# Rope attention: the first two maxima tiles of a step stand between the scores of the two head pairs

## The chip, the cores and the metric

The kernel runs on one core of a Trainium2 chip as one program. The metric is the time of one execution on the device in microseconds (us); before the change it was 4140.08 us (median of three runs, 4134.7 to 4146.66).

## What is computed

Six blocks follow one another on 4 sequences of 1024 tokens of width 128: a feed-forward with rope attention and routed experts, a linear attention, the first kind of feed-forward again, then two mixtures of 14 experts around a causal attention. The change touches the rope attention, which runs twice (blocks one and three). Cut to it:

```
q = (src @ Wq).reshape(Bb, Tt, H, DH).transpose(0, 2, 1, 3)          # H = 16 heads, DH = 8
k = (src @ Wk_c @ Wk).reshape(Bb, Tt, H, DH).transpose(0, 2, 1, 3)
v = (src @ Wv_c @ Wv).reshape(Bb, Tt, H, DH).transpose(0, 2, 1, 3)
q = _apply_rope(q, sin, cos); k = _apply_rope(k, sin, cos)
attn = jnp.einsum('bhqd,bhkd->bhqk', q, k) / np.sqrt(DH)
attn = jax.nn.softmax(attn, axis=-1)
sa = jnp.einsum('bhqk,bhkd->bhqd', attn, v)
```

The softmax needs the largest score of each query before its exponentials; how that maximum is found sets the work around the change.

## The kernel before

`rope_attention` runs 16 iterations (`ITERS`: 4 sequences by 4 groups of 4 heads). The four heads of a group are two pairs. An iteration has 16 steps (`STEPS`): 8 tiles of 128 keys for each half of 512 queries. The second pair runs 8 steps behind the first, so the first 8 steps of iteration 0 have the first pair alone, and 8 steps of the second pair are left after the last iteration.

Per step, TensorE does three kinds of work, in the order in which the program writes it:

- **Scores** (`scores`, L740; matmuls on L745): for each pair two matmuls of 75 rows (split operands and the negated maxima as rows), each 128 keys by 512 queries. They wait until ScalarE has taken the exponentials (L819) of that pair's step before.
- **Weighing** (`weigh`, L748; matmuls on L754): the exponentials of the step before times the values, for four heads, in four column strips of the array at once.
- **Maxima tiles** (`ring`, L722; matmuls on L737): the scores of the iteration ahead once more, this time 128 queries by 512 keys, only so that VectorE can reduce each tile to its row maxima (L877). A step has four, issued as two pairs by `rings` (L759). Of each pair one tile is of an even head (rows 0 to 47 of the array, operands `ra_k`, `ra_q`) and one of an odd head (rows 64 to 111, `ra_ko`, `ra_qo`), so the two can run in the array at the same time.

Maxima tiles go round three PSUM banks (5, 6 and 7). Tile i may be written when VectorE has read tile i-3: `ring` begins with `pe.wait_ge(*been_read(number - 3))`. TensorE works its instructions off in order, so such a wait holds everything behind it.

When a pair's 32 tiles are reduced, VectorE makes one more reduction (L883), and four tiles later TensorE turns the maxima (the transpose on L729, "the turn"), which takes a number in the same ring of banks; ScalarE reads it (L831, L833). There are two turns in an iteration, in step 4 and in step 12, each behind the step's second pair of tiles. They become three rows of `Q` by way of GpSimd and three transfers. The last iteration has tiles in its first four steps only.

In this text S0 and S1 are the scores of the first and of the second pair, A and B the first and the second two maxima tiles of a step, and W the weighing. A's even tile is a, its odd tile is b. In `_(pe)`, before the change, a step is S0, S1, A, W, B:

```
for pair in range(2):
    ...
        scores(n, s, pair, u)
done = rings(n, u, it, done, 2 * s)
...
    weigh((s - 1) % STEPS, u if s else 1 - u, (0, 1) if n or s > KT else (0,))
done = rings(n, u, it, done, 2 * s + 1)
```

Of the kernel before, what the change touches and what calls it, by code (L numbers as in the profile page):

```python
# [533 lines left out]
def rope_attention(nc, g, buffers, sb, sem, project, output_rows):  # L534
# [40 lines left out]
    def halves_of(n):  # L575
        return HALF if n + 1 < ITERS else LAST
# [4 lines left out]
    def ahead(pair, k):  # L581

        return k - KT * pair
# [21 lines left out]
    def been_read(number):  # L605

        return s_bank[number % 3], number // 3 + 1
# [11 lines left out]
    def behind(s, pair, u):  # L619

        if pair == 0:
            return u, s
        return (u if s >= KT else 1 - u), (s - KT) % STEPS
# [9 lines left out]
    with nc.Block() as block:  # L633
# [86 lines left out]
        @block.tensor  # L720
        def _(pe):
            def ring(number, use, n2, u):  # L722


                if number >= 3:
                    pe.wait_ge(*been_read(number - 3))
                if use[0] == "turn":
                    pe.wait_ge(s_mx, n2)
                    pe.transpose(PS[0:PH * KT, 5 + number % 3, 0:P], m[:, use[1], :], IDN[:, :]).then_inc(s_tile, 1)  # L729
                else:  # L730
                    pair, c = use
                    t, h, odd = c // (PH * HALVES), c // PH % HALVES, c % PH
                    if odd:
                        queries, keys = QO[ODD, u, pair, :], KO[ODD, u, pair, :]
                    else:
                        queries, keys = Q[EVEN, u, PH * pair, :], K[EVEN, u, PH * pair, :]
                    pe.matmul(PS[:, 5 + number % 3, :], queries[:, t * P:(t + 1) * P], keys[:, h * BT:(h + 1) * BT],  # L737
                              start=True, stop=True).then_inc(s_tile, 1)

            def scores(n, s, pair, u):  # L740
                ub, step = behind(s, pair, u)
                if ahead(pair, STEPS * n + s):
                    pe.wait_ge(s_exp[pair], ahead(pair, STEPS * n + s))
                for j in (PH * pair, PH * pair + 1):
                    mm = pe.matmul(PS[:, j, :], K[0:KROWS, ub, j, (step % KT) * P:(step % KT + 1) * P],  # L745
                                   Q[0:KROWS, ub, j, (step // KT) * BT:(step // KT + 1) * BT], start=True, stop=True)
                mm.then_inc(s_st[pair], 1)

            def weigh(s, u, pairs=(0, 1)):

                for pair in pairs:
                    ub, step = behind(s, pair, u)
                    for j in (PH * pair, PH * pair + 1):
                        mm = pe.matmul(PS[VW * j:VW * (j + 1), 4, :], VA[:, ub, step % KT, j, :], PR[:, s % 2, j, :],  # L754
                                       start=(s % KT == 0), stop=(s % KT == KT - 1),
                                       skip_group_check=True)
                mm.then_inc(s_pv, 1)

            def rings(n, u, it, done, half):  # L759

                for use in halves_of(n)[half]:
                    if use in (FIRST[0], BEGIN[0]):
                        pe.wait_ge(s_qk[use[0]][1 - u], 16 * LOADS * (it + 1 + u))
                    ring(len(PRO) + len(RING) * n + done, use,
                         2 * n + 2 if use[1] == 1 else 2 * n + 3, u if use in REST else 1 - u)
                    done += 1
                return done

            project.tensor(pe)
            pe.wait_ge(s_qk[0][0], 16 * LOADS)  # L770
            for i, use in enumerate(PRO):
                if use == BEGIN[0]:
                    pe.wait_ge(s_qk[1][0], 16 * LOADS)
                ring(i, use, 1, 0)
            pe.wait_ge(project.s_set, project.SETS)
            pe.wait_ge(project.s_one, 16)
            pe.wait_ge(s_va, 1)
            for it in range(ITERS // 2):
                for u in range(2):
                    n = 2 * it + u  # L780
                    done = 0
                    for s in range(STEPS):
                        for pair in range(2):
                            if s == KT * pair:

                                pe.wait_ge(s_mr[pair][u], 16 * PARTS * (it + 1))
                            if n or s >= KT * pair:
                                scores(n, s, pair, u)
                        done = rings(n, u, it, done, 2 * s)
                        if s % KT == 1 and n + s > 1:  # L790
                            pe.wait_ge(s_of, 2 * n + s // KT)
                        if s == 1:
                            pe.wait_ge(s_va, n + 1)
                        if n or s:
                            weigh((s - 1) % STEPS, u if s else 1 - u, (0, 1) if n or s > KT else (0,))
                        done = rings(n, u, it, done, 2 * s + 1)

            for s in range(KT):
                scores(ITERS, s, 1, 0)
                if s == 1:  # L800
                    pe.wait_ge(s_of, 2 * ITERS)
                weigh((s - 1) % STEPS, 0 if s else 1, (1,) if s else (0, 1))
            pe.wait_ge(s_exp[1], ahead(1, STEPS * ITERS + KT))
            weigh(KT - 1, 0, (1,))
# [2152 lines left out]
```

## Time and profile before

| what | before |
|---|---|
| runs | 4146.66, 4140.08, 4134.7 us; median 4140.08 |
| profiled execution | span 4133.9 us from the first to the last instruction; no time of its own is listed beside it, so what lies around the span is taken from the runs (0.8 us to the fastest, 6.2 us to the median) |
| mean granted TensorE clock | 0.943 |
| busy, share of the span | PE 88%, DVE 75%, ACT 49%, POOL 31% |
| L877 DVE reductions to maxima | 2048, 1309.2 us, mean 686 ns |
| L819 ACT exponentials | 1024, 992.0 us, mean 1019 ns |
| L754 PE weighing | 4096 matmuls (two passes for each fp32 product), mean 606 ns |
| L745 PE scores | 2048 matmuls, mean 383 ns |
| L737 PE maxima tiles | 2 x 1024 matmuls, mean 399 ns |

The two rope attentions have their steps from about 115 to 800 us and from about 1526 to 2200 us of the span. A matmul's row shows its start and a modelled duration that runs on while the next one already starts; so the distance between the starts of two blocks is what a block costs, and the busy column is not. "x4" in a row is four instructions merged, and "[0.36 <-PE ...]" is idle time of the engine before the row and what ended it.

### The profile page before, as it was taken

To read this page: it belongs to the slowest core of one execution; us is meant where nothing else is said; L and a number is where in the kernel's file an instruction comes from. 1 tells how busy PE (TensorE), PEld (TensorE's weight loads), DVE (VectorE), ACT (ScalarE), POOL (GpSimd) and SP (SyncE) were. 2 spreads that over 40 slices of the span, in tenths; PEclk is the share of its full clock that TensorE was granted. 3 is DMA by queue.
4 is the path that set the end of the run, shared out by engine and by line. 5 is a ranking of instruction groups with operands and counts; after the bars stand their busy time and mean duration, and the time that the engine had idled before them with its cause. 6 is when DMAs were issued, how large, how long until landed. Compare 5 with 4: busy or idle time off the path is not lost. (4 is left out here: it accounts for less than half of the span.)

```text
span 4133.9 us, 60386 instructions
## 1 busy us (share of the span) xinstructions
PE 3634.7 (88%) x20845; PEld 1603.4 (39%) x20845; DVE 3108.4 (75%) x7157; ACT 2040.9 (49%) x3136; POOL 1267.6 (31%) x1378
## 2 busy tenths in 40 slices
PE   6999999989888779999998896647999999999865
PEld 2222222254445422222224445533444444444555
DVE  7999999467566699999993785456777777877444
ACT  2577777631343337777775123323444444444433
POOL 1011011011311201101101123434666676676543
PEclk8899999999999879999999997878999999999887
DMA  4211111220200041111115002322000000000133
GB/s 114 60 53 56 55 56 54 91 66 0 77 1 1 12 110 51 55 56 55 54 47 157 1 11 78 88 61 72 2 2 2 2 7 7 2 10 5 43 99 95
DMA packets 330712, 192.85 MB, mean 47 GB/s; under 512 B 172194, under 2 KB 285626, under 8 KB 330410
## 3 DMA queue, kind: packets, MB, share of 16 engines
q1 hardware_dynamic: 314634, 155.93, 14.1%
q0 software_dynamic: 14048, 32.79, 2.7%
q8 instruction: 168, 2.75, 0.3%
q14 instruction: 134, 1.10, 0.1%
q10 hardware_dynamic: 1728, 0.28, 0.0%
HBM read 119.74 MB, written 67.90 MB: 45 GB/s over the span
## 5 line engine op out<-in xcount | busy, mean ns | idle before, releaser
L877 DVE TENSOR_REDUCE ra_mh<-PS 128x1 f32<-128x512 f32 x2048 | 1309.2, 686 | 55.1 <-PE PS L737 34.7
L819 ACT ACTIVATE ra_p<-PS 128x1024 f32<-128x1024 f32 x1024 | 992.0, 1019 | 310.2 <-PE PS L745 309.8
L754 PE MATMUL PS<-ra_p,ra_va 128*32 128x512 f32 x4096 | 565.6, 606 | 0.3
L745 PE MATMUL PS<-ra_q,ra_k 75*128 75x512 bf16 x2048 | 538.5, 383 | 3.8 <-ACT ra_p L819 1.5
L2703 ACT ACTIVATE ca_p<-PS 128x1024 f32<-128x1024 f32 (+3 forms) x384 | 305.2, 811 | 369.6 <-PE PS L2596 366.2
L2774 POOL TENSOR_TENSOR ca_s<-ca_s,ca_p 128x1024 f32<-128x1024 f32 (+3 forms) x256 | 414.7, 1620 | 65.2 <-ACT ca_p L2703 44.5
L737 PE MATMUL PS<-ra_k,ra_q 48*128 48x512 bf16 x1024 | 408.2, 399 | 17.2 <-DMA ra_qo<-q_parts 16.6
L737 PE MATMUL PS<-ra_ko,ra_qo 48*128 48x512 bf16 x1024 | 409.0, 399 | 9.4 <-DVE ra_mh L877 9.4
L737 PEld LDWEIGHTS PS<-ra_k,ra_q 48*128 48x128 bf16 x1024 | 95.0, 93 | 659.3 <-DVE ra_mh L877 374.6
L2592 PE MATMUL PS<-ca_q,ca_k 64*128 64x512 f32 (+3 forms) x1536 | 318.8, 495 | 0.0
L2613 PE MATMUL PS<-ca_p,ca_v 128*64 128x512 f32 (+3 forms) x1536 | 290.3, 498 | 1.6 <-POOL ca_p L2763 1.6
L2823 DVE CUSTOM_DVE_ANT_0 PS<-PS,ca_later 128x128 f32<-128x128 f32 (+3 forms) x512 | 242.1, 514 | 60.5 <-PE PS L2555 54.1
L1146 PE MATMUL PS<-f_w,e_hT 128*128 128x512 f32 x512 | 248.6, 631 | 30.7 <-DVE e_acc L1268 30.7
L745 PEld LDWEIGHTS PS<-ra_q,ra_k 75*128 75x128 bf16 x2048 | 161.0, 98 | 257.1 <-issue 101.9
L706 POOL TENSOR_TENSOR ra_nr<-ra_nm,ra_ko 16x128 f32<-16x128 f32 x64 | 26.8, 419 | 747.3 <-ACT ra_ko L833 747.3
L2176 PE MATMUL PS<-f_xT,f_wb 128*128 128x128 f32 x960 | 147.9, 302 | 118.3 <-issue 42.0
L630 POOL DMA_DIRECT2D o_heads<-rp_rot x122 | 66.0, 543 | 563.1 <-ACT rp_rot L840 563.1
L2307 DVE TENSOR_TENSOR f_yb<-PS,f_b 128x128 f32<-128x128 f32 x240 | 58.4, 285 | 197.3 <-DMA o_heads<-rp_rot 68.8
L2826 DVE TENSOR_REDUCE ca_mh<-PS 128x1 f32<-128x512 f32 x256 | 161.9, 685 | 47.0 <-PE PS L2555 46.7
L2259 POOL DMA_INDIRECT f_yk<-expert_outputs,f_slot x128 | 124.2, 970 | 210.3 <-DMA expert_outputs<-f_yb 92.8
L1268 DVE SCALAR_TENSOR_TENSOR e_acc<-PS,e_w,e_acc 128x128 f32<-128x128 f32 x448 | 157.2, 351 | 35.2 <-PE PS L1146 13.9
L2176 PEld LDWEIGHTS PS<-f_xT,f_wb 128*128 128x128 f32 x960 | 131.5, 212 | 129.9 <-issue 116.4
(270 smaller groups left out, 5654.5 us busy)
## 6 DMA issues: line engine op xcount, KB each, us to landing
ra_k<-k_parts SPq DMA_DIRECT2D x128, 144.0 KB
ra_q<-q_parts SPq DMA_DIRECT2D x128, 144.0 KB
ao_ot<-o_heads SPq DMA_DIRECT2D x16, 1024.0 KB, 9.0
o_heads<-rp_rot POOLq DMA_DIRECT2D x122, 128.0 KB, 4.2
f_xg<-expert_tokens SPq DMA_DIRECT2D x56, 256.0 KB, 3.5
expert_outputs<-f_yb SPq DMA_DIRECT2D x56, 256.0 KB
expert_tokens<-X SPq DMA_DIRECT2D x28, 256.0 KB
q_parts<-rp_parts SPq DMA_DIRECT2D x48, 128.0 KB
```

Source lines behind the costliest of these rows:

```text
L737: pe.matmul(PS[:, 5 + number % 3, :], queries[:, t * P:(t + 1) * P], keys[:, h * BT:(h + 1) * BT], start=True, stop=True).then_inc(s_tile, 1)
L745: mm = pe.matmul(PS[:, j, :], K[0:KROWS, ub, j, (step % KT) * P:(step % KT + 1) * P], Q[0:KROWS, ub, j, (step // KT) * BT:(step // KT + 1) ...
L754: mm = pe.matmul(PS[VW * j:VW * (j + 1), 4, :], VA[:, ub, step % KT, j, :], PR[:, s % 2, j, :], start=(s % KT == 0), stop=(s % KT == KT - ...
L819: act.activation(PR[:, s % 2, PH * pair:PH * (pair + 1), :], PS[:, PH * pair:PH * (pair + 1), :], ACT.Exp, scale=float(DH) ** -0.5).then_i ...
L877: dve.tensor_reduce(mh[:, pair, KT * odd + t, h:h + 1], PS[:, 5 + number % 3, :], AX.X, ALU.max).then_inc(s_bank[number % 3], 1)
L1146: mm = pe.matmul(PS[:, h, :], hT[:, u, FT + f, j * P:(j + 1) * P], w2[:, f, h * EB:(h + 1) * EB, :], start=(f == 0), stop=(f == FT - 1))
L2176: mm = pe.matmul(PS[:, 2 + k % UB, (FT * t + f) * P:(FT * t + f + 1) * P], wb[:, i % WB, f * P:(f + 1) * P], xT[:, c % 2, j * P:(j + 1) * ...
L2592: pe.matmul(PS[:, bank[h], off:BT], K[r, u, kt * P:(kt + 1) * P], Q[r, u, queries], start=True, stop=False)
L2613: mm = pe.matmul(PS[r, 4, off:BT], VA[:, n % 2, kt, r], PR[:, step % SLOTS, h, off:BT], start=(kt == 0), stop=last, skip_group_check=True)
L2703: act.activation(PR[:, step % SLOTS, :, off:BT], PS[:, 2 * (step % 2):2 * (step % 2) + 2, off:BT], ACT.Exp, scale=float(HD) ** -0.5).then_ ...
L2774: pool.tensor_tensor(S[:, qc, :, off:BT], S[:, qc, :, off:BT], new[:, :, off:BT], ALU.add).then_inc(s_sum, 1)
L2823: ins = dve.tensor_tensor_reduce(tile, tile, later[:, BT - width:BT], 1.0, LOWEST, ALU.add, ALU.max, to)
```

## The change

`rings` for the first two tiles of a step moves into the loop over the pairs, behind the scores of the first pair. A step becomes S0, A, S1, W, B. No instruction is added or removed, and no wait: each `ring` keeps its number, its bank and what it waits for.

```diff
@@ -786,7 +786,8 @@
                                 pe.wait_ge(s_mr[pair][u], 16 * PARTS * (it + 1))
                             if n or s >= KT * pair:
                                 scores(n, s, pair, u)
-                        done = rings(n, u, it, done, 2 * s)
+                            if pair == 0:
+                                done = rings(n, u, it, done, 2 * s)
                         if s % KT == 1 and n + s > 1:
                             pe.wait_ge(s_of, 2 * n + s // KT)
                         if s == 1:
```

TensorE's order before, one step of iteration 0 with both pairs (`ra_exp_done0` and `1` are ScalarE's counts of exponentials of the two pairs, `ra_bank_read` VectorE's counts of banks read):

```order
L745 MATMUL PS<-ra_q,ra_k 128x512 [waits ra_exp_done0_5]
L745 MATMUL PS<-ra_q,ra_k 128x512
L745 MATMUL PS<-ra_q,ra_k 128x512 [waits ra_exp_done1_5]
L745 MATMUL PS<-ra_q,ra_k 128x512
L737 MATMUL PS<-ra_k,ra_q 128x512 [waits ra_bank_read1_5]
L737 MATMUL PS<-ra_ko,ra_qo 128x512 [waits ra_bank_read2_5]
L754 MATMUL PS<-ra_p,ra_va 32x512 x4
L737 MATMUL PS<-ra_k,ra_q 128x512 [waits ra_bank_read2_5]
L737 MATMUL PS<-ra_ko,ra_qo 128x512 [waits ra_bank_read0_5]
```

The same step of the changed kernel on TensorE:

```order
L745 MATMUL PS<-ra_q,ra_k 128x512 [waits ra_exp_done0_5]
L745 MATMUL PS<-ra_q,ra_k 128x512
L737 MATMUL PS<-ra_k,ra_q 128x512 [waits ra_bank_read1_5]
L737 MATMUL PS<-ra_ko,ra_qo 128x512 [waits ra_bank_read2_5]
L745 MATMUL PS<-ra_q,ra_k 128x512 [waits ra_exp_done1_5]
L745 MATMUL PS<-ra_q,ra_k 128x512
L754 MATMUL PS<-ra_p,ra_va 32x512 x4
L737 MATMUL PS<-ra_k,ra_q 128x512 [waits ra_bank_read0_5]
L737 MATMUL PS<-ra_ko,ra_qo 128x512 [waits ra_bank_read1_5]
```

Two score matmuls have moved from ahead of A to behind it: A follows the B of the step before at the distance of two matmuls instead of four, and W and B stand farther from A.

At the turn (step 12 of iteration 0), TensorE before:

```order
L729 MATMUL PS<-IDN,ra_m 16x128 [waits ra_m_ready_5,ra_bank_read0_5]
L745 MATMUL PS<-ra_q,ra_k 128x512 [waits ra_exp_done0_5]
L745 MATMUL PS<-ra_q,ra_k 128x512
L745 MATMUL PS<-ra_q,ra_k 128x512 [waits ra_exp_done1_5]
L745 MATMUL PS<-ra_q,ra_k 128x512
L737 MATMUL PS<-ra_k,ra_q 128x512 [waits ra_bank_read1_5]
```

And TensorE there in the changed kernel:

```order
L729 MATMUL PS<-IDN,ra_m 16x128 [waits ra_m_ready_5,ra_bank_read0_5]
L745 MATMUL PS<-ra_q,ra_k 128x512 [waits ra_exp_done0_5]
L745 MATMUL PS<-ra_q,ra_k 128x512
L737 MATMUL PS<-ra_k,ra_q 128x512 [waits ra_bank_read1_5]
L737 MATMUL PS<-ra_ko,ra_qo 128x512 [waits ra_bank_read2_5]
L745 MATMUL PS<-ra_q,ra_k 128x512 [waits ra_exp_done1_5]
```

The first tile behind the turn stands two score matmuls nearer to it.

## Rows read from the trace of the kernel before

**Rows 1.** Stretches: length; busy (x) of PE, PEld, DVE, ACT, POOL; clock, DMA, GB/s.

```profile
200.00:700.00 500.00, 495.75 (x3024) 127.48 (x3026) 482.99 (x774) 387.71 (x456) 51.34 (x117) 1.00 0.19 54
131.00:141.00 10.00, 9.67 (x41) 2.16 (x42) 9.38 (x17) 4.51 (x6) 1.12 (x3) 0.99 0.11 27
```

**Rows 2.** Timeline, PE, one step with both pairs: start, us, engine, line, operation.

```profile
401.80 0.39 PE L737 MATMUL PS<-ra_k,ra_q 48*128 48x512 bf16 x1
401.81 0.39 PE L737 MATMUL PS<-ra_ko,ra_qo 48*128 48x512 bf16 x1
402.12 1.04 PE L745 MATMUL PS<-ra_q,ra_k 75*128 75x512 bf16 x4
403.09 0.39 PE L737 MATMUL PS<-ra_k,ra_q 48*128 48x512 bf16 x1
...
403.41 1.07 PE L754 MATMUL PS<-ra_p,ra_va 128*32 128x512 f32 x8
404.41 0.39 PE L737 MATMUL PS<-ra_k,ra_q 48*128 48x512 bf16 x1
```

**Rows 3.** Timeline, DVE, same step, in narrow windows: starts of single reductions.

```profile
402.83 1.38 DVE L877 TENSOR_REDUCE ra_mh<-PS 128x1 f32<-128x512 f32 x2
...
403.52 1.29 DVE L877 TENSOR_REDUCE ra_mh<-PS 128x1 f32<-128x512 f32 x2
...
404.13 1.40 DVE L877 TENSOR_REDUCE ra_mh<-PS 128x1 f32<-128x512 f32 x2
```

**Rows 4.** Timeline, ahead of the first step: reductions with TensorE waiting for each.

```profile
94.52 9.65 DVE L877 TENSOR_REDUCE ra_mh<-PS 128x1 f32<-128x512 f32 x16
```

**Rows 5.** Timeline, behind the last maxima tile: weighing, then the next scores' weights.

```profile
772.37 1.07 PE L754 MATMUL PS<-ra_p,ra_va 128*32 128x512 f32 x8
773.36 0.55 PEld L745 LDWEIGHTS PS<-ra_q,ra_k 75*128 75x128 bf16 x4 [0.84 <-issue]
```

**Rows 6.** Timeline, PE and DVE, iteration 0: a step with the first pair alone.

```profile
137.84 0.39 PE L737 MATMUL PS<-ra_k,ra_q 48*128 48x512 bf16 x1
...
138.16 0.60 PE L745 MATMUL PS<-ra_q,ra_k 75*128 75x512 bf16 x2
...
138.27 1.29 DVE L877 TENSOR_REDUCE ra_mh<-PS 128x1 f32<-128x512 f32 x2
...
138.70 0.39 PE L737 MATMUL PS<-ra_k,ra_q 48*128 48x512 bf16 x1
139.01 0.39 PE L737 MATMUL PS<-ra_ko,ra_qo 48*128 48x512 bf16 x1
139.33 1.05 PE L754 MATMUL PS<-ra_p,ra_va 128*32 128x512 f32 x4
140.32 0.39 PE L737 MATMUL PS<-ra_k,ra_q 48*128 48x512 bf16 x1
```

**Rows 7.** Timeline, PE and DVE, at a turn with both pairs.

```profile
410.21 0.28 PE L729 MATMUL PS<-IDN,ra_m 128*16 128x128 f32 x1 [0.19 <-DVE ra_mh L877]
...
411.28 0.39 PE L737 MATMUL PS<-ra_k,ra_q 48*128 48x512 bf16 x1
...
411.71 3.42 DVE L877 TENSOR_REDUCE ra_mh<-PS 128x1 f32<-128x512 f32 x5 [0.36 <-PE PS L737]
```

**Rows 8.** Line L883, 200 to 700 us: durations in ns, first and last start.

```profile
L883 DVE TENSOR_REDUCE ra_m<-ra_mh x23: 186/186/189, 216.6 to 686.4; 128x16 f32<-128x32 f32 x23
```

**Rows 9.** Timeline, PE, second attention: scores around a turn, first pair alone.

```profile
1537.96 0.60 PE L745 MATMUL PS<-ra_q,ra_k 75*128 75x512 bf16 x2
...
1540.93 0.60 PE L745 MATMUL PS<-ra_q,ra_k 75*128 75x512 bf16 x2
...
1543.64 0.60 PE L745 MATMUL PS<-ra_q,ra_k 75*128 75x512 bf16 x2
```

**Rows 10.** Timeline, PE, half clock: scores of two steps, first pair alone.

```profile
122.14 1.03 PE L745 MATMUL PS<-ra_q,ra_k 75*128 75x512 bf16 x2
...
126.04 1.03 PE L745 MATMUL PS<-ra_q,ra_k 75*128 75x512 bf16 x2
```

## Prediction

> **What bounds the kernel now.** Only the two rope attentions change, so I read the stretches first, then the timeline of one step engine by engine, and last a place in the same trace where the new order already stands. In the steady stretch VectorE is busy 483.0 of 500 us and TensorE 495.8 [rows 1], so the shares do not decide between the two; the starts do.
>
> On TensorE the blocks of a step follow each other without a gap: B at 401.80, the four scores at 402.12, A at 403.09, W at 403.41, the next B at 404.41 [rows 2]. That is 0.32 for B, 0.97 for S0 with S1, 0.32 for A, 1.00 for W, 2.61 us in all. Each is the block's own length and not a wait: W takes 0.99 (772.37 to 773.36) where the next block waits for nothing but TensorE itself [rows 5], and A and B cost 0.32 each although each is two matmuls, because the two start together (401.80 and 401.81).
>
> VectorE is quicker than it looks. Reductions start at 402.83, 403.52 and 404.13, distances of 0.69 and 0.61 [rows 3]; where TensorE waits for every one of them, sixteen take 9.65 us, (9.65 - 0.68) / 15 = 0.60 each, 0.68 being the length of one (1.29 for two that start 0.61 apart) [rows 3, 4]. So the pair's second reduction follows at VectorE's own 0.605 and the next pair's first is some 0.09 late, twice in a step: 4 x 0.605 = 2.42 us of work in a step of 2.61. TensorE, in its written order, is the bound by a small margin. The page Perfetto Trace Analysis of the Trainium skill (section Identifying the Most-Contended Engine) says the opposite way to read it: occupancy names the bottleneck for the vector engine, while busy matmul time does not measure TensorE. By that rule VectorE at 97% would bind, its four reductions are untouched, and the sum would be nothing lost; the alternating 0.69 and 0.61 speak against it here. It is a rival below.
>
> How a wait on a bank shows itself is in iteration 0, whose first 8 steps have the first pair alone, so that TensorE there already runs S0, A, W, B [rows 6]. B starts at 137.84, S0 at 138.16, a at 138.70, but b only at 139.01, then W at 139.33 and B at 140.32. Tile b may be written when B's even tile has been read. That reduction started at 138.27, 0.43 behind B, and b came 0.74 behind its start. So b can't start sooner than 0.43 + 0.74 = 1.17 us behind B, while S0 alone puts it at 0.32 + 0.54 = 0.86. Tile b comes 0.31 late and, as a has left by then, no longer shares the array with it.
>
> **The change part by part.** Nothing is added or taken out; S1's two matmuls move behind A. With both pairs a step was S0, S1, A, W, B, where A stood 0.32 + 0.97 = 1.29 behind B, just over the 1.17 that b needs [rows 2, 6]. Now A stands 0.86 behind B. The new step, in rows:
>
> - B 0.32 and S0 0.54 (138.16 to 138.70) [rows 6].
> - a, then b 0.31 later, then S1 0.32 behind b [rows 6]; in place of 0.32 for both.
> - S1 0.54. No row shows the second pair's scores alone in a stretch of maxima tiles; it is the same two matmuls as S0, and S0 behind B and ahead of A is the nearest row. The least it could cost is what it adds in a row of four, 0.97 - 0.54 = 0.43 [rows 2, 6].
> - W 0.99 to 1.00 [rows 2, 5].
>
> Sum 0.32 + 0.54 + 0.31 + 0.32 + 0.54 + 0.99 = 3.02; the rows are printed to 0.01, and the same pieces from 2.47 + 0.54 give 3.01. I take 3.01, so 0.40 more than 2.61: 0.11 because four scores in one run (0.97) become two runs (1.08), and 0.29 for the wait of b.
>
> Does the pattern repeat itself? B stands 0.31 + 0.32 + 0.54 + 1.00 = 2.17 behind a, so B's two tiles find their banks read and start together. VectorE has had time to empty the ring, starts on B's even tile 0.43 behind it, and the next b is late by the same 0.31. VectorE's cover of 0.19 in a step grows to 0.6 idle. The other engines have room: ScalarE is busy 387.7 of 500 us, 78% of steps of 2.61 to 2.7 us, and less of longer ones [rows 1]; the loads that SP issues are released by the scores' counts, all of which stretch alike, and no instruction of SP, GpSimd, ScalarE or VectorE changes its place.
>
> How many steps: 15 iterations of 16 and 4 of the last have tiles, less the 8 with the first pair alone, which keep their order: 236 in an attention, 472 in two. 472 x 0.40 = 189 us.
>
> Turns: half an iteration takes (686.4 - 216.6) / 22 = 21.36 us [rows 8], 0.48 more than 8 x 2.61 = 20.88, and that is what a turn costs now. VectorE stands 0.36 idle at it, because the tiles behind the turn wait for four scores (turn at 410.21, tile at 411.28) [rows 7]. S1 behind A removes that cause, but the turn holds a number in the ring, so both tiles behind it depend on a read one place later, 0.605 us: a at B + 1.17 and b at B + 1.78, where an ordinary b has B + 1.17. By that a turn costs 0.605. With the first pair alone, two steps around a turn took 1543.64 - 1537.96 = 5.68, 0.73 over two ordinary ones of 2.475 [rows 9]. So a turn gets dearer by 0.13 to 0.25; 29 turns in an attention fall in affected steps, 58 in all, 7 to 15 us. I take 8, nearer to the replay of the step. The last turn of each attention waits for its maximum ahead of S1 instead of behind: about 0.5 each, 1 us.
>
> Sum 189 + 8 + 1 = 198 us on the span of 4133.9, giving 4332; with the 6.2 us by which the median of the runs lies above the span, 4338.
>
> **Bounds.** With S1 at its least (0.43) the step is 2.90 and the loss 0.29 x 472 + 9 = 146; with b's wait shorter by 0.05 it is 24 us less than forecast; with 0.25 a turn it is 7 more, and a S1 and W dearer by 0.05 together 24 more.
>
> **The rivals.**
>
> - *VectorE is the bound* (chance 0.03). If reductions couldn't follow each other faster than the 0.65 they show on average, the order on TensorE would cost nothing, and the 0.36 idle at a turn would go: 58 x 0.36 = 21 us less, 4119. For it: the 97% [rows 1]. Against it: 0.61 and 0.60 in rows 3 and 4. It decides from the point where 4 reductions need more than TensorE's step, 2.61 of now or 3.01 of then; they need 2.42.
> - *The wait of b is hidden* (0.06), say if S1's weights and matmuls cost no extra behind two separate tiles, or VectorE gives the bank back sooner. Then only the split of the scores is paid: 0.11 x 472 = 52 us, 4192. Against it: b's wait in rows 6, behind the same B and the same two scores.
> - *The ring falls a whole read behind in every step* (0.03), as it does once at a turn: 0.605 more, 472 x 1.005 + 9 = 483 us, 4623. Against it: between a and the next B lie 2.17 us, enough for three reductions.
> - *The clock falls* (0.03). At half clock a step of the first pair takes 3.90 (122.14 to 126.04) against 2.475 [rows 10, 6], 1.58 times; 3.01 becomes 4.74. A tenth of the steps so would add 47 x 1.73 = 81 us, 4419. Against it: 131 to 141 us holds such waits (139.01 is one) at a granted clock of 0.99, the higher level, 2.4 GHz [rows 1]. The page TensorE: Matmul & The Clock Gate of the Trainium skill (Part 1) says that activity releases the clock and idleness takes it back, which is why a waiting TensorE makes this a rival at all; the stretch that holds b's wait does not bear it out.
> - *Nothing comes of it* (0.02): A's move is cancelled by a wait not seen here, 4140.
>
> **How the numbers follow.** My forecast has 0.83. Its own range is 4285 to 4370: down to S1 at its least (4286), up by 24 us for S1 and W and 7 for the turns. As the rivals on both sides hold 0.17 together, the range ends there. About 0.3%, 12 us, is what a measurement of this kernel can tell from no change. Faster by more than that: the first rival, 0.03; within it: the last, 0.02; slower: the rest, 0.95.
>
> **What would show it.** In the profile after, a step with both pairs lasts 3.01 us; a starts 0.86 behind B and b 0.31 behind a, alone; S1 starts 0.32 behind b; L883 stands 24.6 to 24.8 us apart in place of 21.36; VectorE idles some 0.5 us ahead of B's first reduction and its share in 200 to 700 us falls from 97% to about 83%, (3.01 - 0.5) / 3.01; the clock stays where it is. TensorE's busy share hardly falls, as the rows of a and b, 0.39 each, cover the wait. The steps with the first pair alone keep their 2.475. It is wrong if b starts with a, if steps stay at 2.61 to 2.72, or if reductions stay without idle time.

## The result, and the profile after

The changed kernel takes 4344.66 us (median of four runs, 4343.49 to 4347.77) against 4139.92 us (four runs) of the kernel before: 1.0496 times as long, 95% interval 1.0478 to 1.0515. The forecast was 4338. The profiled execution took 4345.34 us with a span of 4343.3, 209.4 more than the span before; the medians lie 204.7 apart.

One step with both pairs in the profile after, as the timeline of TensorE and VectorE has it (start in us, duration in us, engine, line, operation; the reductions' line is L878 now). It answers to [rows 2, 3]:

```profile
400.09 0.39 PE L737 MATMUL PS<-ra_k,ra_q 48*128 48x512 bf16 x1
400.10 0.39 PE L737 MATMUL PS<-ra_ko,ra_qo 48*128 48x512 bf16 x1
...
400.42 0.61 PE L745 MATMUL PS<-ra_q,ra_k 75*128 75x512 bf16 x2
400.52 2.48 DVE L878 TENSOR_REDUCE ra_mh<-PS 128x1 f32<-128x512 f32 x4 [0.54 <-PE PS L737]
...
400.95 0.39 PE L737 MATMUL PS<-ra_k,ra_q 48*128 48x512 bf16 x1
...
401.26 0.39 PE L737 MATMUL PS<-ra_ko,ra_qo 48*128 48x512 bf16 x1
...
401.58 0.60 PE L745 MATMUL PS<-ra_q,ra_k 75*128 75x512 bf16 x2
...
402.12 1.06 PE L754 MATMUL PS<-ra_p,ra_va 128*32 128x512 f32 x8
...
403.12 0.39 PE L737 MATMUL PS<-ra_k,ra_q 48*128 48x512 bf16 x1
```

Read the starts. B at 400.09, S0 0.33 later, a at 400.95 (0.86 behind B), b not before 401.26 (1.17 behind B, 0.74 behind the start of the reduction of B's even tile at 400.52), S1 0.32 behind b, W 0.54 behind S1, the next B 1.00 behind W: 3.03 us in place of 2.61. VectorE does its four reductions in one run of 2.48 and then stands idle for 0.54.

The stretches and the spacing of the maxima (answers to [rows 1, 8]); in the first two rows the columns are the stretch, its length, busy time and count of PE, PEld, DVE, ACT and POOL, the granted clock, the DMA share and GB/s:

```profile
200.00:700.00 500.00, 492.98 (x2603) 109.27 (x2606) 404.71 (x667) 353.49 (x394) 43.76 (x100) 1.00 0.16 46
131.00:141.00 10.00, 9.97 (x34) 1.86 (x33) 7.84 (x14) 3.60 (x5) 1.11 (x3) 0.74 0.01 2
```

```profile
L884 DVE TENSOR_REDUCE ra_m<-ra_mh x20: 186/186/188, 206.5 to 677.7; 128x16 f32<-128x32 f32 x20
```

VectorE's share fell from 97% to 81%, TensorE's stayed at 99%: a row of 0.39 us for a and another for b cover the wait between them. The clock of the steady stretch is 1.00 as before; in 131 to 141 us, in the start-up of the first attention, it is 0.74 instead of 0.99. Half an iteration takes (677.7 - 206.5) / 19 = 24.80 us instead of 21.36.

The turn after, TensorE and VectorE (answers to [rows 7]):

```profile
406.14 0.39 PE L737 MATMUL PS<-ra_k,ra_q 48*128 48x512 bf16 x1
...
406.46 0.28 PE L729 MATMUL PS<-IDN,ra_m 128*16 128x128 f32 x1
...
407.31 0.39 PE L737 MATMUL PS<-ra_k,ra_q 48*128 48x512 bf16 x1
...
407.91 0.39 PE L737 MATMUL PS<-ra_ko,ra_qo 48*128 48x512 bf16 x1 [0.21 <-DVE ra_mh L878]
...
410.19 2.49 DVE L878 TENSOR_REDUCE ra_mh<-PS 128x1 f32<-128x512 f32 x4 [1.14 <-PE PS L737]
```

Both tiles behind the turn come one read later: a 1.17 and b 1.77 behind B. Here b is 0.60 behind a, TensorE stands idle for 0.21 ahead of it, and the next scores start 0.92 behind a.

### The profile page after: what moved, and what is told of

Its sections match the earlier page's. It is cut to its first block and busy times, and to the rows that moved or that the text cites. A ratio compares the mean times of both kernels' runs of the same rounds, so it can differ in the third digit from the quotient of the medians.

```text
span 4343.3 us, 60386 instructions
## 1 busy us (share of the span) xinstructions
PE 3833.5 (88%) x20845; PEld 1608.1 (37%) x20845; DVE 3074.4 (71%) x7157; ACT 2097.7 (48%) x3136; POOL 1264.7 (29%) x1378
## 5 line engine op out<-in xcount | busy, mean ns | idle before, releaser
L878 DVE TENSOR_REDUCE ra_mh<-PS 128x1 f32<-128x512 f32 x2048 | 1276.2, 683 | 294.4 <-PE PS L737 294.1
L820 ACT ACTIVATE ra_p<-PS 128x1024 f32<-128x1024 f32 x1024 | 1043.7, 1022 | 462.7 <-PE PS L745 401.8
L745 PE MATMUL PS<-ra_q,ra_k 75*128 75x512 bf16 x2048 | 621.6, 386 | 3.9 <-ACT ra_p L820 1.5
L745 PEld LDWEIGHTS PS<-ra_q,ra_k 75*128 75x128 bf16 x2048 | 122.6, 98 | 251.8 <-issue 208.9
```

The source lines that it names most:

```text
L820: act.activation(PR[:, s % 2, PH * pair:PH * (pair + 1), :], PS[:, PH * pair:PH * (pair + 1), :], ACT.Exp, scale=float(DH) ** -0.5).then_i ...
L878: dve.tensor_reduce(mh[:, pair, KT * odd + t, h:h + 1], PS[:, 5 + number % 3, :], AX.X, ALU.max).then_inc(s_bank[number % 3], 1)
```

## The experiments

All four ran beside the kernel before (median 4140.7 us in these runs).

**Before's order, short reductions.**

```diff
-                dve.tensor_reduce(mh[:, pair, KT * odd + t, h:h + 1], PS[:, 5 + number % 3, :],
+                dve.tensor_reduce(mh[:, pair, KT * odd + t, h:h + 1], PS[:, 5 + number % 3, 0:BT // 4],
```

> The order of before; each maxima tile is still computed over 512 keys, but VectorE reduces 128 of them only (the maximum is taken over a quarter of the keys). Theory (TensorE's written order is the bound, VectorE has slack): the step stays 2.61 us although the reductions shrink from 0.60 to some 0.20 us; only a turn gets cheaper, from 0.48 to about 0.11, so 60 x 0.37 = 22 us less: about 4118, between 4105 and 4135. Rival (VectorE binds at 97% busy): steps shrink with the reductions, by 0.3 us or more, 472 x 0.3 = 140 us or more: under 4000.

Measured: 4115.28 us (4106.19 to 4123.69), ratio 0.9924 (0.9897 to 0.9950). The timeline of TensorE and VectorE, an ordinary step, then the stretch of 500 us and the spacing of the maxima:

```profile
405.90 0.39 PE L737 MATMUL PS<-ra_k,ra_q 48*128 48x512 bf16 x1
...
406.32 0.49 DVE L877 TENSOR_REDUCE ra_mh<-PS 128x1 f32<-128x128 f32 x2 [0.83 <-PE PS L737]
...
407.19 0.39 PE L737 MATMUL PS<-ra_k,ra_q 48*128 48x512 bf16 x1
...
408.51 0.39 PE L737 MATMUL PS<-ra_k,ra_q 48*128 48x512 bf16 x1
```

```profile
200.00:700.00 500.00, 500.00 (x3078) 127.55 (x3078) 190.64 (x786) 394.91 (x466) 52.61 (x120) 1.00 0.19 55
```

```profile
L883 DVE TENSOR_REDUCE ra_m<-ra_mh x24: 185/186/188, 212.7 to 695.3; 128x16 f32<-128x32 f32 x24
```

VectorE's share falls from 97% to 38%, and the step stays 405.90 to 408.51, 2.61 us. What goes is the turn: half an iteration takes (695.3 - 212.7) / 23 = 20.98, so a turn costs 0.10 instead of 0.48. With that, the rival in which VectorE bound the steps of the kernel before has fallen by experiment: TensorE's written order bound them. Only at a turn did the length of the reductions count, with 0.38 of its 0.48.

**After's order, short reductions.** The same edit on the changed kernel.

> The order of after, with the same short reductions (128 keys of 512). The reduction of B's first tile then ends some 0.33 us behind its start, so its bank is free 0.77 us behind B's start, ahead of the 0.86 at which tile b is due. Theory (the loss is 0.31 for b's wait and 0.11 for splitting the four scores in two runs): a and b start together, the step is 2.61 + 0.11 = 2.72, and this kernel lies 472 x 0.11 = 52 us above the one with before's order and short reads: about 4170, between 4155 and 4190. Rival (the loss is in the order on TensorE itself, not in the wait): it stays about 200 us above, 4320.

Measured: 4164.24 us (4158.29 to 4167.39), ratio to before 1.0050 (1.0034 to 1.0067), 49 us above the kernel with before's order and the same reductions. The timeline of TensorE and VectorE, one step:

```profile
403.32 0.39 PE L737 MATMUL PS<-ra_k,ra_q 48*128 48x512 bf16 x1
...
403.65 0.61 PE L745 MATMUL PS<-ra_q,ra_k 75*128 75x512 bf16 x2
...
403.75 0.49 DVE L878 TENSOR_REDUCE ra_mh<-PS 128x1 f32<-128x128 f32 x2 [1.37 <-PE PS L737]
...
404.19 0.39 PE L737 MATMUL PS<-ra_k,ra_q 48*128 48x512 bf16 x1
404.19 0.39 PE L737 MATMUL PS<-ra_ko,ra_qo 48*128 48x512 bf16 x1
404.51 0.61 PE L745 MATMUL PS<-ra_q,ra_k 75*128 75x512 bf16 x2
405.04 1.07 PE L754 MATMUL PS<-ra_p,ra_va 128*32 128x512 f32 x8
406.04 0.39 PE L737 MATMUL PS<-ra_k,ra_q 48*128 48x512 bf16 x1
```

The reduction of B's even tile starts at 403.75, and a short one lasts 0.28, so its bank is free in time: b starts together with a at 404.19, and the step is 2.72: only the split of the four scores is paid, 0.11 of the 0.42. The other 0.31 is b's wait, shown by taking away its cause, the length of the reduction.

**The two tiles apart.** Order S0, a, S1, b, W, B, by handing `rings` one tile at a time:

```diff
-            def rings(n, u, it, done, half):
+            def rings(n, u, it, done, half, part=slice(None)):
-                for use in halves_of(n)[half]:
+                for use in halves_of(n)[half][part]:
...
-                        done = rings(n, u, it, done, 2 * s)
+                            done = rings(n, u, it, done, 2 * s, slice(pair, pair + 1))
```

> Order S0, a, S1, b, W, B: the even tile behind the first pair's scores, the odd one behind the second pair's. Tile b is then due 1.72 us behind B, later than the 1.17 from which its bank is free, so it waits for nothing. Theory (a late b costs because it no longer shares the array with a): b takes 0.32 of its own, the step is 0.325 + 0.535 + 0.32 + 0.535 + 0.32 + 1.00 = 3.035, as long as that of after: about 4350, between 4330 and 4370. Rival (the price is TensorE standing still at the wait): without a wait the step is 2.72 to 2.83, 4192 to 4245.

Measured: 4331.99 us (4327.98 to 4342.51), ratio 1.0460 (1.0430 to 1.0490). TensorE's timeline:

```profile
404.27 0.39 PE L737 MATMUL PS<-ra_k,ra_q 48*128 48x512 bf16 x1
...
405.13 0.39 PE L737 MATMUL PS<-ra_k,ra_q 48*128 48x512 bf16 x1
405.45 0.61 PE L745 MATMUL PS<-ra_q,ra_k 75*128 75x512 bf16 x2
405.99 0.39 PE L737 MATMUL PS<-ra_ko,ra_qo 48*128 48x512 bf16 x1
406.30 1.07 PE L754 MATMUL PS<-ra_p,ra_va 128*32 128x512 f32 x8
407.30 0.39 PE L737 MATMUL PS<-ra_k,ra_q 48*128 48x512 bf16 x1
```

The step is 3.03, as long as in the changed kernel, although b stands 1.72 behind B and waits for nothing. It pays 0.31 of its own (405.99 to 406.30) where a shared pair pays 0.32 for two. So the wait as such is not the price; what costs is that b no longer shares the array with a. The kernel is 13 us under the changed one because a turn is cheaper: half an iteration from this kernel's row,

```profile
L883 DVE TENSOR_REDUCE ra_m<-ra_mh x21: 185/186/189, 203.2 to 694.4; 128x16 f32<-128x32 f32 x21
```

(694.4 - 203.2) / 20 = 24.56, less 8 x 3.03 = 24.24, is 0.32 a turn where the changed kernel pays 0.60; 58 x 0.28 = 16 us less for turns and some 2 us more for steps (3.03 against 3.025) make 14 us. The expectation had left turns out and named 4350; its range began at 4330.

**A between the two heads of S1.** Order S0, the first matmul of S1, A, its second matmul, W, B. `scores` is told which of a pair's two matmuls to issue (one line more in it, so the weighing stands on L755):

```diff
-            def scores(n, s, pair, u):
+            def scores(n, s, pair, u, heads=(0, 1)):
...
-                for j in (PH * pair, PH * pair + 1):
+                for j in [PH * pair + h for h in heads]:
...
-                                scores(n, s, pair, u)
+                                scores(n, s, pair, u, (0,) if pair else (0, 1))
                         done = rings(n, u, it, done, 2 * s)
+                        if n or s >= KT:
+                            scores(n, s, 1, u, (1,))
```

> Order S0, first matmul of S1, A, second matmul of S1, W, B: A stands 0.325 + 0.755 = 1.08 us behind B, 0.09 short of the 1.17 that b needs. Theory (b is late by what lacks to 1.17, and a late b still shares the array for the rest of a): the step is 2.61 + 0.11 for the split run + 0.09 = 2.81, 472 x 0.20 = 94 us more: about 4234, between 4215 and 4260. Rival 1 (a b that is late at all shares nothing and costs a whole 0.31): the step is about 3.03, 4340. Rival 2 (the needed distance is under 1.08): 2.72, 4192.

Measured: 4242.01 us (4239.44 to 4246.22), ratio 1.0239 (1.0213 to 1.0265). TensorE's timeline, and the spacing of the maxima:

```profile
404.76 0.39 PE L737 MATMUL PS<-ra_k,ra_q 48*128 48x512 bf16 x1
...
405.08 0.82 PE L745 MATMUL PS<-ra_q,ra_k 75*128 75x512 bf16 x3
405.84 0.39 PE L737 MATMUL PS<-ra_k,ra_q 48*128 48x512 bf16 x1
405.93 0.39 PE L737 MATMUL PS<-ra_ko,ra_qo 48*128 48x512 bf16 x1
406.25 0.39 PE L745 MATMUL PS<-ra_q,ra_k 75*128 75x512 bf16 x1
406.57 1.06 PE L755 MATMUL PS<-ra_p,ra_va 128*32 128x512 f32 x8
407.57 0.39 PE L737 MATMUL PS<-ra_k,ra_q 48*128 48x512 bf16 x1
```

```profile
L886 DVE TENSOR_REDUCE ra_m<-ra_mh x21: 185/186/188, 222.0 to 683.3; 128x16 f32<-128x32 f32 x21
```

a is due 1.08 behind B, b comes at 1.17, and the step is 2.81. Lateness is paid in proportion, 0.09 here and 0.31 in the changed kernel, and the earliest start of b, 1.17 behind B, is the same in both. That matters, because in the changed kernel alone 0.31 is also what a takes by itself: there a b that waits for its bank and a b that simply runs behind a look the same. Here b starts 0.09 behind a, the next scores 0.41 behind a (405.84 to 406.25), and so the 1.17 is the bank's, and a late b still shares the array for the rest. The loss, 101 us, is 472 x 0.20 = 94 for the steps and some 6 for the turns: (683.3 - 222.0) / 20 = 23.07, less 8 x 2.81 = 22.48, is 0.59 instead of 0.48.

None of these runs points to an order that beats the kernel before: each leaves its step at 2.61 or lengthens it, and the one that is faster does less work on VectorE.

## Why the prediction was right

- **The bound.** TensorE's written order, not VectorE at 97%: shown by the short reductions, which took VectorE to 38% and left the step at 2.61.
- **The step.** Forecast 3.01, measured 3.025 (two steps from 400.09 to 406.14 in the profile after are 6.05). The terms: splitting the scores 0.11, as forecast, shown alone by the second experiment; b's wait 0.31, where the sum had taken 0.29 to meet the lower of its two readings (3.02 and 3.01). 472 x 0.415 = 196 us instead of 189.
- **b's earliest start.** 1.17 us behind B, from a step of the kernel before that happened to run in the new order [rows 6]: found again to 0.01 in the changed kernel and in the fourth experiment, which alone shows that the bank sets it and not the end of a.
- **The turn.** Forecast 0.605 from the ring's shift by one read; measured 24.80 - 8 x 3.025 = 0.60, against 0.48 before. 58 x 0.12 = 7 us, forecast 8.
- **The sum.** 196 + 7 + 1 = 204, against 204.7 between the medians and 209.4 between the two profiled spans. The 1 for the last turns is in the trace as well: from the last maxima tiles to the last scores of an attention it is 39.36 us (874.32 to 913.68) instead of 38.93 (770.09 to 809.02), and the same in the second. From the first scores to the last of each attention the starts lie 103 us farther apart than before, 206.5 in both. What that is above the sum comes from the start-up, which the forecast had unchanged: the first eight steps, with the first pair alone and in the same order in both kernels, take 2.6 us more, 26.52 and 23.99 us (116.83 to 143.35, 1629.59 to 1653.58) instead of 25.30 and 22.60 (115.34 to 140.64, 1525.99 to 1548.59). Each attention does one step more at the lower clock, 1.2 GHz: in the first one the granted clock was 0.50 up to 131 us before and up to 136 us after, with TensorE at work almost without a break in both. No run shows what moved its rise. The other 3 us lie outside the attentions, in stages that the change leaves as they were, and within the 12 us over which the runs spread.
- **Where luck helped.** The forecast of the span, 4332, missed by 11 us, that of the median only by 7. The 6.2 us that the forecast put between the two came from a profiled execution that was faster than the middle of its runs; after the change the median lies 1.4 us above the profiled span (4344.66 against 4343.3).
- **The rivals.** The wait hidden: it was not, and the price named for it, 52 us, is what was measured (49) once its cause was taken away. A whole read behind in every step: no, a waits for nothing except at a turn. The clock: 1.00 in the steady stretch before and after, so it did not fall; it only rose later in the start-up, which cost 2.6 us and not 81. VectorE idle ahead of B's first reduction: 0.54, forecast 0.5; its share 81%, forecast 83%.

## What to carry to other kernels

When two engines hand tiles through a small ring, look at the distance between visits and not at the busy shares: here, with three banks and tiles in pairs, a visit may not follow the one before sooner than write (0.43) plus read and release (0.74), and an order with visits at 1.29 and 1.32 just kept that where one at 0.86 and 2.17 did not, with the same work. And before guessing what a new order costs, look for a place in the old trace where it already runs: a start-up stretch with the first pair alone gave b's wait and most other terms of this sum; S1 had to be taken from S0, and W from a full step.

## What was not expected

The prediction had only the one case in which b comes as a has left. What lies around it came out of the experiments: a late partner of a pair that shares the array costs what it is late. 0.09 late cost 0.09 and 0.31 late cost 0.31; at the turn of the changed kernel b is 0.60 late, part of it with TensorE idle, and the pair costs 0.92 instead of 0.32. Moved away altogether, with other work in between, b cost 0.31 and no more.

Three scores in a run cost 0.76, two 0.54, one 0.32: about 0.22 each, with 0.11 for every run. That is why four scores cost 0.11 more in two runs than in one; what makes up the 0.11 no run shows.
